# Attention of a dense masked transformer layer: scores of two heads at a time on the two halves of the array's rows, in place of one head on all 128

## The chip, the cores and the metric

The kernel runs on one core of one Trainium2 chip. The time is the device time of one execution in microseconds (us), and the number compared is the median of several runs. The core has a tensor engine (PE; its weight loads are listed apart as PEld), a vector engine (DVE), a scalar engine (ACT), GpSimd (POOL) and a queue (SP) that issues the DMAs. Each of them works off its own list of instructions in order, and they wait for one another by semaphores.

## What is computed

A graph attention network of two layers over 1250 nodes, then a graph transformer of two layers over the same edges. The change lies in the transformer. Cut to what matters:

```
N, D, H, DH, L = 1250, 512, 8, 64, 2
for l in range(L):
    q = ((x @ Wq[l].T + bq[l]) * scaling).reshape(n, H, DH)
    k = (x @ Wk[l].T).reshape(n, H, DH)
    v = (x @ Wv[l].T).reshape(n, H, DH)
    scores = jnp.einsum('ehd,ehd->eh', q[tgt], k[srcidx])
    m = segment_max(scores, tgt);  p = jnp.exp(scores - m[tgt])
    w = p / (segment_sum(p, tgt)[tgt] + 1e-16)
    agg = segment_sum(w[:, :, None] * v[srcidx], tgt)
    attn = agg.reshape(n, D) @ Wo[l].T + bo[l]
    x = _batchnorm(x + attn, ...)
    ff = relu(x @ W1[l].T + b1[l]) @ W2[l].T + b2[l]
    x = _batchnorm(x + ff, ...)
```

The kernel does not go edge by edge. It computes all 1250 x 1250 scores of a head and adds a matrix of logarithms of edge counts (`logs`, very negative where there is no edge), so that the softmax over all nodes is the softmax over the edges.

## The kernel before

**Stages.** A front stage counts edges, a stage computes the graph attention, and then each transformer layer has two stages: `stage_project_attend` (projections of x to k, q and v, then attention) and `stage_tail` (output projection, feed-forward, norms). A final stage normalises. In the profiled execution the projections of layer 0 run from 790 to 878 us and its attention from 878 to 1166 us; for layer 1 the attention runs from 1324 to 1612 us. The two attentions are the same program on other data.

**Two-part numbers.** A product that needs more precision than one pass gives is made of `high` and `low` parts (F32R each). Attention before the change uses the 64 channels of a head twice: `k_halves` holds k_high of a head in one half of the 128 partitions and k_low in the other (for odd heads the other way round), `q_first` and `q` (shown as `q_att` in the profile) hold q_high, copied to both halves of the partitions, and q_low, likewise. A matmul over all 128 rows then gives q_part·(k_high + k_low), and two of them, over q_high and q_low, give the score.

**Getting there.** `project_parts` works through five chunks of 250 nodes: k (48 matmuls), q (48), v (24). `save_k` (L1690) writes k_high by two copies of 64 partitions, `cut_k` (L1811) makes k_low by two subtractions, and SP stores k_low into the other half of the partitions (`store_k`). q goes out to the DRAM tensor `q_rows` (`store_q`) and comes back duplicated and reordered (`q_first_loaded`; later chunks by `load_q` in `attend_sync`).

**Attention.** A unit u is one head of one tile of 125 target nodes; there are 80 units a layer, two in a row make a pair p, 40 pairs a layer. For each unit:

- `score(u)` on PE (L2019): three column pieces of 512, 512 and 226 keys, twice, into three PSUM banks that all units share. It waits until unit u-1 is masked.
- `mask(u)` on DVE (L2125): reads the scores, adds `logs`, writes `probs`, and takes the row maximum.
- `exponential(u)` on ACT (L2073), then `safe` (L2130) and `divide` (L2134, L2136) on DVE.
- `turn(u)` on PE (L2029): ten transposes of 125 x 125 in three pieces of 4, 3 and 3, each piece into one bank. Before the change four banks go round (`RING = 4`, banks 3 to 6); a piece waits until the copy has emptied the bank of the piece four back.
- `save_turned(u)` on ACT (L2081): three copies out of these banks.
- `weigh(p)` on PE (L2040): for each of ten tiles one matmul for each of the pair's two heads, 64 weights' columns each, the even head into PSUM partitions 0 to 63 and the odd one into 64 to 127 of bank 7. The profile lists each of these F32 matmuls as two records, 40 a pair.
- `save_att(p)` on ACT (L2088) copies the result out.

The order on each engine is written out by hand. On PE it is turn(2p), turn(2p+1), score(2p+4), weigh(p-1), score(2p+5); DVE masks unit u+1 before it divides unit u; ACT does save_turned of both units, exponentials of units 2p+3 and 2p+4, save_att(p-1). On ACT and DVE eight cuts of the next stage's weights (`cut_w` L2094, `lower_w` L2142) are spread over pairs 16 to 30.

Of the kernel before, what the change touches and what calls it, by code (L numbers as in the profile page):

```python
# [1421 lines left out]
class LayerBuffers:  # L1422


    def __init__(self, k, ctx, gat, base, hidden):
# [6 lines left out]
        self.k_halves = base  # L1432
        self.q_out = base + 4 * H * N
        self.wk = gat.HIDDEN
        self.x_high = self.wk + 2 * weight
        self.x_low, self.k_low = self.x_high + x_size, self.x_high + 2 * x_size
        self.y, self.v_rows = gat.ROWS, gat.ROWS + gat.HALF
        self.q_first = gat.ROWS + 2 * gat.HALF
        self.wq = self.q_first + 8 * H * W
# [3 lines left out]
        self.w1, self.wo = self.q_out, self.x_high  # L1443
        self.w2 = self.wo + 2 * weight
        self.bias_rows = self.w1 + 8 * C * F * 128
        self.q_second = self.wk
# [23 lines left out]
def project_parts(k, ctx, places, x, x_cols, sources, weights, ready, loaded, bq, q_rows, q_first, k_halves, v_rows, logs, log_rows,  # L1470
# [18 lines left out]
    q_out = at("q_out", [128, 2, C, W], F32R, places.q_out)  # L1489
    k_low = at("k_low", [128, 2, C, W], F32R, places.k_low)  # L1490
# [6 lines left out]
    k.q_stored = nc.alloc_semaphore(f"q_stored{k.layer}")  # L1497
    k_stored = [k.sem(f"k_stored{slot}_qkv{k.layer}") for slot in range(2)]
    x_stored, prefetched = k.sem(f"x_stored_qkv{k.layer}"), k.sem(f"prefetched_qkv{k.layer}")
    q_first_loaded = k.sem(f"q_first_loaded_qkv{k.layer}")  # L1500
# [12 lines left out]
    k.q_saved, k.k_summed, k.k_low_done, k.v_summed, k.v_saved, k.k_stored = q_saved, k_summed, k_low_done, v_summed, v_saved, k_stored  # L1513
    k.q_first_loaded, k.first_logs_loaded, k.cols_stored = q_first_loaded, prefetched, x_stored
# [9 lines left out]
    def v_bank(t):  # L1524
        return k.psum[0:P, (4 + t) * BANK:(5 + t) * BANK]
# [7 lines left out]
    def own(odd):  # L1533
        return slice(odd * CH, (odd + 1) * CH)

    def nodes(s):
        return slice(s * W, (s + 1) * W)

    def k_at(rows, odd, s):
        return k_halves[own(rows)].rearrange("p (c odd) n -> p odd c n", odd=2)[:, odd][:, :, nodes(s)]  # L1540

    def project_sync(sp):
# [15 lines left out]
        def store_k(r):  # L1558
            sp.wait_ge(k_low_done, r + 1)
            for odd in range(2):  # L1560
                sp.dma_start(k_at(1 - odd, odd, r).bitcast(F32), k_low[own(odd), r % 2].bitcast(F32)
                             ).then_inc(k_stored[r % 2], 16)

        def store_q(r):
# [10 lines left out]
        if closing:  # L1575
            for t in range(A):
                store_rows(t)
        store_k(0)
        store_q(0)
        if closing:  # L1580
            for t in LATE:
                store_rows(t)
# [1241 lines left out]
```

## Time and profile before

| | |
|---|---|
| median of 3 runs | 1726.2 us (1725.1 to 1726.7) |
| span of the profiled execution | 1723.2 us |
| PE busy | 1572.0 us (91%) |
| DVE busy | 1300.9 us (75%) |
| ACT busy | 1177.9 us (68%) |
| POOL busy | 55.2 us (3%) |
| mean granted TensorE clock | 0.962 |

The profiled execution has a span of 1723.2 us from its first to its last instruction, 3.0 us less than the median of the timed runs; what lies around it is start and end of the program. How to read it: "busy" is time in which an engine has at least one instruction in it, and for PE the ends of matmuls are modelled, so starts of matmuls are what to measure by. The granted clock is a share of 2.4 GHz. A row of the timeline merges instructions of one kind that follow each other ("x20"); its first number is the start of the first.

### The profile page before, as it was taken

The page shows a single profiled execution, that of the slowest core. Times are in us where ns is not written, and L with a number is a line of the kernel's source. Part 1 is how long each engine was busy: PE and PEld are TensorE (multiplying, and loading weights), DVE is VectorE, ACT ScalarE, POOL GpSimd, SP SyncE. Part 2 cuts the span into 40 slices and gives each one's busy share as a digit, 9 for nine tenths or more (in the row PEclk, how much of TensorE's full clock was granted, in tenths as well). Part 3 has the DMA queues.
Part 4 walks back from the last instruction along what each step waited for, and adds up shares of the span by engine and source line. Part 5 has one row for each costly group of instructions (what it writes and reads, how often), then busy time and mean ns, then how long its engine had stood idle before and what let it go on. Part 6 is the DMA issues. An engine that isn't in the chain of part 4 may idle for free. (4 is left out here: it accounts for less than half of the span.)

```text
span 1723.2 us, 35023 instructions
## 1 busy us (share of the span) xinstructions
PE 1572.0 (91%) x14122; PEld 1429.3 (83%) x14122; DVE 1300.9 (75%) x2269; ACT 1177.9 (68%) x2181; POOL 55.2 (3%) x67
## 2 busy tenths in 40 slices
PE   7899799999995888798989999998799999999982
PEld 3788799999975777787978888888798888888882
DVE  6996999989468999995357777766733777777577
ACT  3455788888656999896457788873434777887434
POOL 0000000000000100000001000001100000000030
PEclk9899899999997999899999999999899999999995
DMA  4113222300006321112955333004067333200501
GB/s 180 55 53 101 83 70 76 122 31 2 1 1 176 120 91 61 61 32 86 245 151 150 91 89 85 16 2 134 1 158 205 94 78 78 64 2 1 123 5 59
DMA packets 76435, 139.33 MB, mean 81 GB/s; under 512 B 16849, under 2 KB 50353, under 8 KB 74992
## 3 DMA queue, kind: packets, MB, share of 16 engines
q1 hardware_dynamic: 76272, 137.06, 28.2%
q8 instruction: 114, 1.87, 0.5%
q14 instruction: 49, 0.40, 0.1%
HBM read 96.22 MB, written 29.45 MB: 73 GB/s over the span
## 5 line engine op out<-in xcount | busy, mean ns | idle before, releaser
L2125 DVE CUSTOM_DVE_ANT_0 probs_att<-banks,logs_or_y 125x1250 f32<-125x1250 f32 x160 | 233.6, 1460 | 124.9 <-PE banks L2019 123.5
L1028 PE MATMUL banks<-ident,probs_gat 125*125 125x125 f32 x1600 | 214.1, 283 | 46.7 <-ACT probs_gat L1132 46.1
L2081 ACT COPY probs_t_att<-banks 125x375 f32<-125x375 f32 (+1 forms) x480 | 205.0, 532 | 72.1 <-PE banks L2029 72.1
L2073 ACT ACTIVATE probs_att<-probs_att,neg_max_att 125x1250 f32<-125x1250 f32 x160 | 218.4, 1365 | 48.5 <-DVE neg_max_att L2125 48.5
L1028 PEld LDWEIGHTS banks<-ident,probs_gat 125*125 125x125 f32 x1600 | 194.7, 195 | 57.3 <-ACT probs_gat L1132 57.1
L1132 ACT ACTIVATE probs_gat<-probs_gat,neg_max_gat 125x1250 f32<-125x1250 f32 x160 | 214.7, 1342 | 34.3 <-DVE neg_max_gat L1301 33.8
L1301 DVE CUSTOM_DVE_ANT_0 probs_gat<-probs_gat,log_counts 125x1250 f32<-125x1250 f32 x160 | 236.8, 1480 | 0.1
L2040 PE MATMUL banks<-probs_t_att,v_rows 125*64 125x125 f32 x3200 | 189.5, 272 | 0.9 <-ACT feature_cols L2088 0.9
L2029 PE MATMUL banks<-ident,probs_att 125*125 125x125 f32 x1600 | 189.3, 273 | 0.0
L1039 PE MATMUL banks<-h,probs_t_gat 125*125 125x128 f32 x1600 | 188.9, 274 | 0.0
L2040 PEld LDWEIGHTS banks<-probs_t_att,v_rows 125*64 125x64 f32 x3200 | 170.6, 136 | 19.5 <-ACT probs_t_att L2081 17.7
L2029 PEld LDWEIGHTS banks<-ident,probs_att 125*125 125x125 f32 x1600 | 181.3, 189 | 4.7 <-DVE probs_att L2136 0.3
L1039 PEld LDWEIGHTS banks<-h,probs_t_gat 125*125 125x125 f32 x1600 | 182.1, 189 | 0.0
L2136 DVE TENSOR_SCALAR probs_att<-probs_att,inverse_att 125x1250 f32<-125x1250 f32 x160 | 140.1, 876 | 5.6
L1143 ACT COPY probs_t_gat<-banks 125x1250 f32<-125x1250 f32 x120 | 142.9, 1191 | 1.0 <-PE banks L1028 0.7
L2019 PE MATMUL banks<-k_halves,q_first 128*125 128x512 f32 (+1 forms) x576 | 134.3, 368 | 9.4 <-DVE neg_max_att L2125 7.9
L1295 DVE SCALAR_TENSOR_TENSOR probs_gat<-a_pair,a_dst_gap 125x1250 f32<-125x1250 f32 x80 | 121.3, 1517 | 21.5 <-PE banks L1028 12.0
L1295 DVE SCALAR_TENSOR_TENSOR probs_gat<-a_pair,a_dst_gap_gat 125x1250 f32<-125x1250 f32 x80 | 120.8, 1511 | 8.8 <-DMA a_pair<-a_src_rows 5.7
L2019 PEld LDWEIGHTS banks<-k_halves,q_first 128*125 128x125 f32 x576 | 92.7, 187 | 32.7 <-DVE neg_max_att L2125 9.9
L2019 PE MATMUL banks<-k_halves,q_att 128*125 128x512 f32 (+1 forms) x384 | 89.6, 368 | 0.0
L547 PEld LDWEIGHTS banks<-offset_hot,key_hot_fr 125*125 125x125 bf16 x650 | 76.0, 143 | 15.6 <-DVE offset_hot L361 7.0
L547 PE MATMUL banks<-offset_hot,key_hot_fr 125*125 125x250 bf16 x650 | 81.7, 280 | 7.2 <-issue 7.1
(258 smaller groups left out, 2892.9 us busy)
## 6 DMA issues: line engine op xcount, KB each, us to landing
a_pair<-a_src_rows SPq DMA_DIRECT2D x46, 625.0 KB, 4.8
q_first<-q_rows SPq DMA_DIRECT2D x12, 1000.0 KB, 11.2
logs_or_y<-log_rows SPq DMA_DIRECT2D x20, 546.9 KB
q_rows<-q_out_qkv SPq DMA_DIRECT2D x40, 250.0 KB, 4.6
q_att<-q_rows SPq DMA_DIRECT2D x8, 1000.0 KB, 10.8
w_rows<-in_L_gnn_W_dram SPq DMA_DIRECT2D x12, 512.0 KB, 13.7
log_counts<-counts_fr SPq DMA_DIRECT2D x50, 122.1 KB
k_halves<-k_low_qkv SPq DMA_DIRECT2D x20, 250.0 KB, 3.9
```

The source lines that it names most:

```text
L547: product = pe.matmul(sums(g), key_hot[:, g % 2, r, 0:P], offset_hot[:, (first[g] + r) % RING], start=r == 0, stop=r == R - 1)
L1028: block_t = pe.transpose(turned(u)[:, i // 2, (i % 2) * P:(i % 2 + 1) * P], probs[:, u % PROBS, i * P:(i + 1) * P], k.ident[0:P, 0:P])
L1039: total = pe.matmul(out_bank(u), probs_t_slot(u)[:, i], rows, start=i == 0, stop=i == T - 1)
L1132: act.activation(probs[:, u % PROBS], probs[:, u % PROBS], ACT.Exp, scale=-1.0, bias=neg_max[:, column(u)], accum_out=sums[:, column(u)]). ...
L1295: dve.scalar_tensor_tensor(probs[:, u % PROBS], gat.pair[0:P, head % 2, 0], (gat.gap1, gap2)[layer][:, t, head:head + 1], gat.pair[0:P, he ...
L1301: dve.tensor_tensor_reduce(probs[:, u % PROBS], probs[:, u % PROBS], k.log_counts[:, t], -1.0, -FLOOR, ALU.add, ALU.min, neg_max[:, column ...
L2019: total = pe.matmul(scores[:, a:a + width], q[r % 2][:, h, half, t % 2 * P:(t % 2 + 1) * P], k_halves[:, h, a:a + width], start=half == 0, ...
L2029: block_t = pe.transpose(turned(u, j)[:, (i - lo) * P:(i - lo + 1) * P], probs[:, u % SLOTS, i * P:(i + 1) * P], k.ident[0:P, 0:P])
L2040: total = pe.matmul(out_bank[odd * CH:(odd + 1) * CH], v_rows[:, i, h * CH:(h + 1) * CH], probs_t[:, u % TURNED, i], start=i == 0, stop=i ...
L2073: act.activation(probs[:, u % SLOTS], probs[:, u % SLOTS], ACT.Exp, scale=-1.0, bias=neg_max[:, column(u)], accum_out=sums[:, column(u)]). ...
L2081: act.copy(probs_t[:, u % TURNED, lo:hi].rearrange("p c n -> p (c n)"), turned(u, j)).then_inc(piece_saved, 1)
L2125: dve.tensor_tensor_reduce(probs[:, u % SLOTS], scores, logs[:, t % KEPT], -1.0, -FLOOR, ALU.add, ALU.min, neg_max[:, column(u)]).then_inc ...
```

## The change

The score of a pair is computed at once, by 18 matmuls over 64 rows each: the nine of the even head read partitions 0 to 63, the nine of the odd head partitions 64 to 127. They are q_high·k_high, q_high·k_low and q_low·k_high for each of three column pieces (q_low·k_low is no longer computed). The scores of a pair take 2500 columns, five banks; the odd head's pieces are 512, 452 and 286 wide, the even head's 226, 512 and 512, and the two share bank 2 (`shared_done` keeps the odd head's matmuls out of it until the even head's are done). The matmuls of the two heads are listed by the column at which each would begin if both heads streamed side by side.

k_high, k_low and q_high, q_low now stay where ACT and DVE write them, as [128, C, nodes]: a pair's two heads are already the two halves of the partitions. So `store_k`, `store_q`, the reload of q and their semaphores go, `save_k` and `cut_k` are one instruction each, and each chunk of q has a place of its own (`q_chunks`).

The three banks that are left (5, 6, 7) go round among seven tenants a pair: the six pieces of transposes and the result of `weigh`. A piece of an odd unit waits until the same piece of the even unit is copied out.

```
@@ attend_parts
-        def score(u):
...
-            for half in range(2):
-                for a, width in pieces(N):
-                    total = pe.matmul(scores[:, a:a + width], q[r % 2][:, h, half, t % 2 * P:(t % 2 + 1) * P],
-                                      k_halves[:, h, a:a + width], start=half == 0, stop=half == 1)
+        def score(p):
+            t, c = p // PER_TILE, p % PER_TILE
+            halves = q_chunks[t // 2][:, :, c, t % 2 * P:(t % 2 + 1) * P]
+            if p >= 1:
+                pe.wait_ge(masked, 2 * p)
...
+            for _, o, a, b, i in sorted(streams):
+                half, keys = ((0, k_high), (0, k_low), (1, k_high))[i]
+                if o == 1 and i == 0 and (a, b) == odd[-1]:
+                    pe.wait_ge(shared_done, p + 1)
+                total = pe.matmul(k.psum[0:P, a:b], halves[own(o), half], keys[own(o), c, a - o * N:b - o * N],
+                                  start=i == 0, stop=i == 2)
...
         def turn(u):
+            q, odd = u // 2, u % 2
             pe.wait_ge(divided, u + 1)
             for j, (lo, hi) in enumerate(CUTS):
-                if u * PIECES + j >= RING:
-                    pe.wait_ge(piece_saved, u * PIECES + j - RING + 1)
+                if odd:
+                    pe.wait_ge(piece_saved, 2 * q * PIECES + j + 1)
+                elif j < PIECES - 1 and q >= 1:
+                    pe.wait_ge(piece_saved, (2 * q - 1) * PIECES + j + 2)
+                elif q >= 2:
+                    pe.wait_ge(att_saved, q - 1)
...
         def weigh(p):
-            pe.wait_ge(piece_saved, (2 * p + 2) * PIECES)
-            if p >= 1:
-                pe.wait_ge(att_saved, p)
+            pe.wait_ge(piece_saved, (2 * p + 2) * PIECES + (PIECES + 1 if p + 1 < PAIRS else 0))
...
+        for p in range(PAIRS + 2):
+            if p < PAIRS:
+                score(p)
+            if p == 0:
+                by_rows(CHUNKS - 1, (1,))
...
+            if 1 <= p <= PAIRS:
+                turn(2 * p - 2)
+                turn(2 * p - 1)
+            if p >= 2:
+                weigh(p - 2)
@@ attend_scalar: save_turned(2p-2), save_turned(2p-1), exponential(2p), save_att(p-2), exponential(2p+1), cut_w
@@ attend_vector
+        for p in range(PAIRS):
+            mask(2 * p)
+            mask(2 * p + 1)
+            if p - 1 in cut_at:
+                lower_w(cut_at[p - 1])
+            for u in (2 * p, 2 * p + 1):
+                safe(u)
+                divide(u)
@@ project_parts
-            for odd in range(2):
-                saved = act.copy(like_banks(k_at(odd, odd, s)), by_feature(0)[own(odd)])
-            saved.then_inc(k_high_done, 1)
+            act.copy(like_banks(k_high[:, :, nodes(s)]), by_feature(0)).then_inc(k_high_done, 1)
```

The first score now also waits until the last chunk's q_low is made (`k.q_low_done`). The weights of the next stage are loaded in two parts (`rows_loaded` for Wo and W1 once eight pairs are scored, `last_rows_loaded` for W2 once 32 are), because W2 takes the place of a chunk of q; six cuts stand at pairs 16 to 26, two at pairs 35 and 36.

One pair on PE in the middle of a layer, before the change (L2029 turn, L2019 score, L2040 weigh):

```order
L2029 MATMUL banks<-ident,probs_att_10469 125x125 x3
L2029 MATMUL banks<-ident,probs_att_10469 125x125 [waits piece_saved_att0]
L2029 MATMUL banks<-ident,probs_att_10469 125x125 x2
L2029 MATMUL banks<-ident,probs_att_10469 125x125 [waits piece_saved_att0]
L2029 MATMUL banks<-ident,probs_att_10469 125x125 x2
L2019 MATMUL banks<-k_halves_10449,q_first_10452 125x512 [waits masked_att0]
L2019 MATMUL banks<-k_halves_10449,q_first_10452 125x512
L2019 MATMUL banks<-k_halves_10449,q_first_10452 125x226
L2019 MATMUL banks<-k_halves_10449,q_first_10452 125x512 x2
L2019 MATMUL banks<-k_halves_10449,q_first_10452 125x226
L2040 MATMUL banks<-probs_t_att_10470,v_rows_10450 64x125 [waits att_saved_att0,piece_saved_att0]
L2040 MATMUL banks<-probs_t_att_10470,v_rows_10450 64x125 x19
```

The end of a pair's scores and the beginning of the transposes behind them on PE with the change (L1982 score, L1999 turn):

```order
L1982 MATMUL banks<-k_high_10449,q_chunk_0_10453 125x286 [waits shared_done_att0]
L1982 MATMUL banks<-k_low_10450,q_chunk_0_10453 125x286
L1982 MATMUL banks<-k_high_10449,q_chunk_0_10453 125x512
L1982 MATMUL banks<-k_high_10449,q_chunk_0_10453 125x286
L1999 MATMUL banks<-ident,probs_att_10471 125x125 [waits divided_att0,total_step_fr]
L1999 MATMUL banks<-ident,probs_att_10471 125x125 x9
L1999 MATMUL banks<-ident,probs_att_10471 125x125 [waits piece_saved_att0,divided_att0]
L1999 MATMUL banks<-ident,probs_att_10471 125x125 x3
L1999 MATMUL banks<-ident,probs_att_10471 125x125 [waits piece_saved_att0]
```

Here it is the first pair, whose even unit finds all banks empty; the odd unit's first transpose waits for two semaphores, `divided` and `piece_saved`. Scores stood between the transposes and the weighing before; now all 20 transposes of a pair stand in a row, with the 20 matmuls of the weighing straight behind them.

Two units on DVE, before:

```order
L2125 ISA probs_att_10469,neg_max_att<-banks,logs_or_y_10451 125x1250 [waits piece_turned_att0,scored_att0]
L2125 ISA neg_max_att 125x1
L2130 TENSOR_SCALAR sums_safe_att<-sums_att 125x1 [waits exp_done_att0]
L2134 RECIPROCAL inverse_att<-sums_safe_att 125x1 [waits sum_safe_att0]
L2136 TENSOR_SCALAR probs_att_10469<-probs_att_10469,inverse_att 125x1250 [waits inverted_att0]
L2125 ISA probs_att_10469,neg_max_att<-banks,logs_or_y_10451 125x1250 [waits piece_turned_att0,scored_att0]
L2125 ISA neg_max_att 125x1
```

and with the change:

```order
L2084 ISA probs_att_10471,neg_max_att<-banks,logs_or_y_10452 125x1250 [waits piece_turned_att0,scored_att0]
L2084 ISA neg_max_att 125x1
L2084 ISA probs_att_10471,neg_max_att<-banks,logs_or_y_10452 125x1250 [waits piece_turned_att0,scored_att0]
L2084 ISA neg_max_att 125x1
L2089 TENSOR_SCALAR sums_safe_att<-sums_att 125x1 [waits exp_done_att0]
L2093 RECIPROCAL inverse_att<-sums_safe_att 125x1 [waits sum_safe_att0]
L2095 TENSOR_SCALAR probs_att_10471<-probs_att_10471,inverse_att 125x1250 [waits inverted_att0]
```

The two masks of a pair stand together, and the divisions of both units come behind them.

## Rows read from the trace of the kernel before

**Rows 1.** Busy by stretch: us; PE, PEld, DVE, ACT, POOL; clock; DMA; GB/s

```profile
20.00:45.00 25.00, 21.98 (x131) 13.71 (x129) 15.46 (x20) 12.65 (x31) 0.00 (x0) 1.00 0.19 57
810.00:850.00 40.00, 40.00 (x296) 37.55 (x295) 21.67 (x34) 21.69 (x35) 0.00 (x0) 1.00 0.71 172
899.00:1161.00 262.00, 262.00 (x2721) 234.77 (x2722) 196.76 (x381) 209.23 (x423) 16.12 (x18) 1.00 0.29 73
```

**Rows 2.** Timeline of PE, one pair (start us, us, engine, line, what, count)

```profile
936.17 1.42 PE L2019 MATMUL banks<-k_halves,q_att 128*125 128x512 f32 x6
937.42 2.35 PE L2029 MATMUL banks<-ident,probs_att 125*125 125x125 f32 x20
939.53 1.37 PE L2019 MATMUL banks<-k_halves,q_att 128*125 128x512 f32 x6
940.83 2.37 PE L2040 MATMUL banks<-probs_t_att,v_rows 125*64 125x125 f32 x40
943.13 1.42 PE L2019 MATMUL banks<-k_halves,q_att 128*125 128x512 f32 x6
```

**Rows 3.** Timeline of PE, beginning and end of layer 0's attention

```profile
878.51 1.42 PE L2019 MATMUL banks<-k_halves,q_first 128*125 128x512 f32 x6 [0.79 <-issue]
...
899.00 0.32 PE L2040 MATMUL banks<-probs_t_att,v_rows 125*64 125x125 f32 x1
...
1150.16 2.37 PE L2040 MATMUL banks<-probs_t_att,v_rows 125*64 125x125 f32 x40
```

**Rows 4.** Timelines of ACT and DVE in that pair

```profile
938.12 2.56 ACT L2081 COPY probs_t_att<-banks 125x500 f32<-125x500 f32 x6 [1.05 <-PE banks L2029]
940.51 1.39 ACT L2073 ACTIVATE probs_att<-probs_att,neg_max_att 125x1250 f32<-125x1250 f32 x1
...
937.62 1.46 DVE L2125 CUSTOM_DVE_ANT_0 probs_att<-banks,logs_or_y 125x1250 f32<-125x1250 f32 x1 [1.01 <-PE banks L2019]
```

**Rows 5.** Timeline of PE: an F32 matmul alone, and two on column halves

```profile
24.12 3.63 PE L573 MATMUL banks<-feature_cols,wa_fr 128*40 128x512 f32 x8
...
1045.61 0.33 PE L2040 MATMUL banks<-probs_t_att,v_rows 125*64 125x125 f32 x2
```

**Rows 6.** PE: starts of single matmuls, and one line's weight loads (min/median/max ns)

```profile
877.09 0.40 PE L1644 MATMUL banks<-wv_low,x_high_qkv 128*125 128x512 f32 x1
877.32 0.40 PE L1644 MATMUL banks<-wv_high,x_low_qkv 128*125 128x512 f32 x1
...
936.50 0.39 PE L2019 MATMUL banks<-k_halves,q_att 128*125 128x512 f32 x1
...
1160.71 0.27 PE L2029 MATMUL banks<-ident,probs_att 125*125 125x125 f32 x1
1160.91 0.33 PE L2040 MATMUL banks<-probs_t_att,v_rows 125*64 125x125 f32 x2
...
L580 PEld LDWEIGHTS banks<-ident,a_turned x10: 178/184/184, 37.5 to 38.5; 8*125 8x125 f32 x10
```

**Rows 7.** Timelines of PE, ACT and DVE where one waits for another

```profile
1158.29 0.37 PE L2029 MATMUL banks<-ident,probs_att 125*125 125x125 f32 x1
...
1159.08 0.58 ACT L2081 COPY probs_t_att<-banks 125x500 f32<-125x500 f32 x1 [0.41 <-PE banks L2029]
...
1158.70 0.87 DVE L2136 TENSOR_SCALAR probs_att<-probs_att,inverse_att 125x1250 f32<-125x1250 f32 x1
...
1159.63 0.37 PE L2029 MATMUL banks<-ident,probs_att 125*125 125x125 f32 x1
...
1163.33 0.26 ACT L2088 COPY feature_cols<-banks 128x125 f32<-128x125 f32 x1 [1.58 <-PE banks L2040]
...
1163.74 0.51 PE L2040 MATMUL banks<-probs_t_att,v_rows 125*64 125x125 f32 x5 [0.45 <-ACT feature_cols L2088]
```

**Rows 8.** DVE at the last chunk of q, and a DMA row (KB each, us to landing)

```profile
877.67 1.20 DVE L1817 TENSOR_TENSOR q_out_qkv<-q_qkv,q_out_qkv 128x1000 fp32r<-128x1000 f32 x1 [3.82 <-ACT q_out_qkv L1705]
...
q_first<-q_rows SPq DMA_DIRECT2D x12, 1000.0 KB, 11.2
```

More of the change, by code:

```diff
@@ L1907, in attend_parts @@
     PAIRS = UNITS // 2
+    PER_TILE, PER_CHUNK = H // 2, H
     KEPT = 4
@@ L1937, in attend_parts, with scores, columns, ring @@
         cuts += [(rows, high, low, a, a + step) for a in range(0, rows.shape[1], step)]
-    scored, masked, exp_done, sum_safe, inverted, divided, piece_turned, piece_saved, summed, att_saved = (
-        k.sem(f"{what}_att{k.layer}") for what in ("scored", "masked", "exp_done", "sum_safe", "inverted", "divided",
-                                          "piece_turned", "piece_saved", "summed", "att_saved"))
-    scores = k.psum[0:P, 0:N]
+    late = weights[-1][0].shape[1] * weights[-1][0].shape[2] // BANK
+    cut_at = {2 * PER_CHUNK + 2 * i: i for i in range(len(cuts) - late)}
+    cut_at.update({(CHUNKS - 1) * PER_CHUNK + 3 + i: len(cuts) - late + i for i in range(late)})
+    shared_done, scored, masked, exp_done, sum_safe, inverted, divided, piece_turned, piece_saved, summed, att_saved = (
+        k.sem(f"{what}_att{k.layer}") for what in ("shared_done", "scored", "masked", "exp_done", "sum_safe", "inverted", "divided",
+                                          "piece_turned", "piece_saved", "summed", "att_saved"))
+    def scores(odd):
+        return k.psum[0:P, odd * N:(odd + 1) * N]
+    def columns(odd):
+        lo, hi = odd * N, (odd + 1) * N
+        edges = [lo] + [b for b in range(0, 8 * BANK, BANK) if lo < b < hi] + [hi]
+        found = list(zip(edges, edges[1:]))
+        return found[-1:] + found[:-1] if odd == 0 else found[1:] + found[:1]
+    def ring(pair, tenant):
+        return (5 + (pair * TENANTS + tenant) % 3) * BANK
     def turned(u, j):
         lo, hi = CUTS[j]
-        at = (3 + (u * PIECES + j) % RING) * BANK
+        at = ring(u // 2, u % 2 * PIECES + j)
         return k.psum[0:P, at:at + (hi - lo) * P]
-    out_bank = k.psum[:, 7 * BANK:7 * BANK + P]
+    def out_bank(p):
+        at = ring(p + 1, 2 * PIECES)
+        return k.psum[:, at:at + P]
     def tile_of(u):
         return u // H
+    def own(odd):
+        return slice(odd * CH, (odd + 1) * CH)
     def column(u):
@@ L1957, in attend_sync @@
     def attend_sync(sp):
-        def load_q(r):
-            if r == 1:
-                sp.wait_ge(k.q_stored, 64 * (T // 2))
-                sp.wait_ge(k.k_summed, CHUNKS)
-            if r >= 2:
-                sp.wait_ge(scored, (r - 1) * 2 * H)
-            for copy in range(2):
-                sp.dma_start(q[r % 2][copy * CH:(copy + 1) * CH].bitcast(F32), q_rows[r]).then_inc(q_loaded[r % 2], 16)
         def load_logs(t):
@@ L2765, in build @@
                 sources = [[w[name][i] for name in ("Wk", "Wq", "Wv")] for i in range(layer, min(layer + 2, layers))]
-                k_halves = places.at(f"k_halves{layer}", [2 * CH, H, N], F32R, places.k_halves)
+                k_high, k_low = (places.at(f"k_{half}{layer}", [128, C, N], F32R, place)
+                                 for half, place in (("high", places.k_high), ("low", places.k_low)))
                 v_rows = places.at(f"v_rows{layer}", [P, T, D], F32, places.v_rows)
```

222 lines of the change are left out of this document (74 added, 148 removed).

## Prediction

> **What bounds the kernel now.** The page names PE the busiest engine at 91%, so I first asked for the busy time by stretch. In the attention of layer 0 PE is busy for 262.00 of 262.00 us while ACT is busy for 209 and DVE for 197, and in the projections for 40.00 of 40.00 us, ACT and DVE for some 22 each [rows 1]. The clock is granted in full (1.00, so 2.4 GHz) in both. Then the timeline of PE gives one pair by the starts of its phases [rows 2]: score 936.17 to 937.42 (1.25 us), 20 transposes to 939.53 (2.11), score to 940.83 (1.30), weighing to 943.13 (2.30), 6.96 in all. From the first weighing (899.00) to the one 36 pairs on (1150.16) it is 251.16 / 36 = 6.98 a pair [rows 3]. No phase waits: before the change attention costs what PE's list costs. A microsecond off PE counts only as far as PE does not begin to wait, since per pair ACT needs 209.23 / 262 x 6.98 = 5.6 us and DVE 5.2.
>
> **The change, part by part.**
>
> *Scores.* A pair has 2 x 2 x 1250 = 5000 columns to stream before, 1.25 + 1.30 = 2.55 us. Now it is 3 x 1250 = 3750 for each head, if the two heads stream side by side. No row of this trace has two matmuls on halves of the rows. The nearest is the weighing, two heads on halves of the columns. Eight F32 records of 512 columns, one at a time at the full clock, take 3.63 us [rows 1, 5], 0.45 each at most, so one of 125 columns would take 0.105 or a little more; 40 of them alone would be 4.2 us. The weighing's 40 take 2.30 [rows 2], and two start within the same 0.01 us [rows 5]. Halves of the columns do run side by side. From above the bound is no overlap at all, from below full overlap without any cost per matmul. I take full overlap with today's cost per matmul: 0.23 us for 512 columns and, where a matmul is short, 0.11, the distance of weight loads (877.09 to 877.32; ten loads in 1.0 us) [rows 6]. The even head has six of 512 and three of 226: 6 x 0.232 + 3 x 0.11 = 1.72. The odd head (512, 452, 286, three each) comes to the same by 0.45 ns a column, 1.70. A first matmul behind a change of the array's use costs 0.10 more (936.17 to 936.50 is 0.33, not 0.23), and so does the first behind a wait. Such a change also costs 0.09 ahead of it (1160.71 to 1160.91 is 0.20, where transposes are 0.11 apart) [rows 2, 6]. Before the change scores and transposes used the array alike; now they do not, so there are three changes a pair in place of two. Score phase: 1.72 + 0.10 + 0.09 = **1.91**, against 2.55: 0.64 less.
>
> *Transposes.* Twenty of them take 2.11 now. With three banks in place of four the odd unit's first piece waits until the even unit's first piece is copied out. From the first transpose behind a change to the beginning of that copy it is 0.79 (1158.29 to 1159.08), the copy takes 0.58 [rows 7], and PE goes on 0.15 later when, as here, it has two semaphores to wait for (the copy ends at 1163.59, PE starts at 1163.74), 0.06 when it has one (1159.57 to 1159.63) [rows 7]. So the odd unit starts 0.79 + 0.58 + 0.15 = 1.52 after the even one, where PE had been ready after ten transposes, 1.19. Then the weighing waits for the copy of the odd unit's first piece, since that bank is where its result goes: 0.79 + 0.58 + 0.06 = 1.43 more. **2.95** in place of 2.11: 0.84 more. Other pieces don't wait: the third bank's copies follow at 0.4 us each [rows 4], ahead of PE.
>
> *Weighing.* Twenty matmuls as before, **2.30**. It is no longer between two scores, but the change of use on either side is in it as before.
>
> *A pair.* 1.91 + 2.95 + 2.30 = **7.16** against 6.98, 0.18 more. Is another engine late? The second loop is weighing, copy of its result, exponential of the odd unit (behind that copy on ACT), its division, its transposes: 2.30 + about 0.25, 1.4 to 1.5, some 1.3 for the division (0.87 and two small instructions ahead of it), 0.06, and then 1.43 until the next weighing, 6.8 [rows 4, 7]. That is 0.35 less than 7.16, so it does not decide, but it is a floor: no gain in the scores can bring a pair under 6.8. The masks (1.46 each) lie beside the transposes.
>
> *Start of a layer.* Now 899.00 - 878.51 = 20.49 from the first score to the first weighing [rows 3]. The first score begins 0.4 later, since it waits for the last q_low, ready at 878.87 [rows 8]. Then, from it: scores 1.8; the last v, 12 matmuls of 0.23, until 4.7, its copy to 5.5; odd unit's exponential to 7.0 and division to 8.3; the masks of the next pair behind it on DVE, to 11.1; third scores to 13.0, beside them the exponentials and divisions to 14.3; transposes and copy 1.5: first weighing at 16.0. So 4.1 less a layer.
>
> *End of a layer.* Before, the last weighing starts 1163.74 - 878.51 = 285.23 after the first score [rows 3, 7]. With the change: 0.4 + 16.0 + 37 x 7.16 + 6.8 (the pair without scores, on the second loop) + 2.3 = 290.4. **5.2 us more a layer**, most of it 37 x 0.18 = 6.7, less 4.1 at the start, plus 2.6 at the end, where the pairs without scores used to be short.
>
> *At nothing:* one copy and one subtraction of k in place of two each, and the stores of k and q: PE is busy throughout the projections [rows 1], and if that cover went, ACT would save 1 us a chunk. The reload of q (12 DMAs of 1000 KB, 11.2 us each) [rows 8], since PE waits for nothing in a pair. The cuts of weights, eight a layer: 512 columns each, so about a copy's 0.58, and ACT has 7.16 - 5.6 = 1.5 us a pair to spare, most of it ahead of the first copy, DVE more behind its masks; uncovered they would be 8 x 0.6 = 5 us a layer. The first four tiles of the edge matrix are asked for no later than before, so the first mask does not wait for them.
>
> *Sum.* Two layers, 2 x 5.2 = 10: 1723.2 becomes 1733 in a profiled execution; the median stands 3.0 above the profiled span, so **1736**.
>
> **What decides.** Equal time needs 7.02 a pair, a score phase of 1.77. A measurement can tell 0.2%, 3.45 us or 0.05 a pair, from no change: below 1.72 it is faster, above 1.82 slower. My 1.91 is made of a borrowed cost per matmul.
>
> **Rivals.**
>
> *Faster: the halves hide each other's costs.* The 0.02 per matmul beyond its columns and the 0.10 of the first fall away when the other half streams: 3750 columns at 2.4 GHz are 1.56, and 0.09 gives 1.65. It speaks for this that the weighing's pairs of matmuls have next to no such cost (2.30 for 20 x 0.105). 0.26 x 37 x 2 = 19 less: 1717.
>
> *No change.* Half of that: a score phase of 1.72 to 1.82, or the waits for copies a tenth shorter: 1723 to 1730, say 1727.
>
> *Slower still: weight loads of the two halves go one behind the other.* 18 loads 0.11 apart are 1.98 in place of 1.72 [rows 6], 0.26 x 37 x 2 = 19 more: 1755. Against it: column halves load 0.01 apart. The Trainium skill ("TensorE: Matmul & The Clock Gate", Part 3, packing small matmuls) has four matmuls on quarters of the rows 3.07 times as fast as one by one, not 4; taken over as an estimate, 1.72 x 4 / 3.07 = 2.24 and the time some 1775. No run here shows that yet.
>
> *It does not do what it says:* matmuls on row halves run one after another. 1.72 + 1.70 = 3.42, 1.70 more for each of 40 pairs of two layers: 1736 + 136 = 1872. Only that column halves overlap speaks against it.
>
> **Chances.** Forecast (1730 to 1746) 0.45; faster 0.20; no change 0.17; serial loads 0.11; no overlap 0.07. So faster 0.20, same 0.17, slower 0.63. The range takes in both 1717 and 1755 with a little round them, 1713 to 1758, and leaves out no overlap and the tails, about 0.15.
>
> **What would show it.** The phases of a pair by their starts on PE: scores 1.9 until the first transpose, transposes 2.95 until the weighing, 2.3. A new wait of PE for ACT's copies (L1999 and L2008 for probs_t) of 0.3 + 0.15 a pair. Odd and even matmuls starting side by side in the scores. The first weighing 16 after the first score. I am wrong if scores take under 1.75 or over 2.0, or if PE takes the 20 transposes in under 2.7.

## Result: 0.3% to 0.6% slower, from the waits that were forecast, and less than was forecast

The changed kernel takes 1728.5 us (median of 20 runs, 1725.2 to 1734.5) beside 1725.2 us (20 runs) of the kernel before: the ratio is **1.0029, 95% interval 1.0019 to 1.0039**, so 5.0 us slower (3.3 to 6.7); the two medians are 3.3 us apart. One of the 20 runs of the kernel before took 2040.6 us and is left out of the ratio. Two later comparisons of the same two programs gave 1.0057 and 1.0046 (below). The forecast was 1736 us, 9.8 above the median shown before, a ratio of 1.0057, with a range of 1730 to 1746 (1713 to 1758 with the nearer rivals). The sign and the mechanism came true, the amount did not: 1728.5 lies under the 1730 to 1746 and inside the 1723 to 1730 that the prediction gave to "no change", and 5.0 us is half of the 9.8. The two later comparisons lie nearer to the forecast ratio, one of them on it.

The profiled execution of the changed kernel has a span of 1723.6 us, 0.4 more than before. That can't be read as "no change": the part of the program ahead of the first projection, which the change doesn't touch, took 785.5 us in this execution and 791.8 in that of before. From the first projection matmul to the end it is 938.1 against 931.4 us, 6.7 more. So I compare the changed stages with each other.

The busy time by stretch of the changed kernel (us; PE, PEld, DVE, ACT, POOL; clock; DMA; GB/s), projections and then attention, for [rows 1]:

```profile
810.00:850.00 40.00, 40.00 (x300) 37.73 (x300) 13.69 (x17) 17.55 (x28) 0.00 (x0) 1.00 0.39 105
890.00:1145.00 255.00, 247.02 (x2796) 222.23 (x2793) 189.20 (x367) 203.21 (x402) 13.84 (x16) 1.00 0.14 41
```

PE was busy in all of its time before; now 8 of 255 us are open, at the same full clock. In the projections DVE works 13.7 us of 40 in place of 21.7 and DMA's share halves, and PE's 40.00 show that this was worth nothing. Where the 8 us lie is seen in the timeline of PE, one pair, for [rows 2]:

```profile
934.34 0.49 PE L1982 MATMUL banks<-k_high,q_chunk 64*125 64x226 f32 x2
934.54 0.27 PE L1982 MATMUL banks<-k_low,q_chunk 64*125 64x226 f32 x1
...
935.93 0.39 PE L1982 MATMUL banks<-k_high,q_chunk 64*125 64x512 f32 x2
936.25 1.35 PE L1999 MATMUL banks<-ident,probs_att 125*125 125x125 f32 x10
937.76 1.32 PE L1999 MATMUL banks<-ident,probs_att 125*125 125x125 f32 x10 [0.16 <-ACT probs_t_att L2040]
939.15 2.37 PE L2008 MATMUL banks<-probs_t_att,v_rows 125*64 125x125 f32 x40
941.45 0.50 PE L1982 MATMUL banks<-k_high,q_chunk 64*125 64x226 f32 x2
```

Scores 934.34 to 936.25 (1.91), transposes to 939.15 (2.90), weighing to 941.45 (2.30): 7.11, and 7.12 as the median of all. The transposes are now two rows with a gap in front of the second, put down to ACT's copies. Those copies on ACT's timeline, for [rows 7]:

```profile
937.04 1.33 ACT L2040 COPY probs_t_att<-banks 125x500 f32<-125x500 f32 x3 [1.00 <-PE banks L1999]
938.52 1.32 ACT L2040 COPY probs_t_att<-banks 125x500 f32<-125x500 f32 x3 [0.15 <-PE banks L1999]
```

The first copy begins 0.79 us after the first transpose (936.25 to 937.04) and PE goes on 0.72 after that; the odd unit's copies begin 0.76 after 937.76, and the weighing 0.63 after them. The beginning and the end of layer 0's attention on PE, for [rows 3]:

```profile
871.73 0.40 PE L1599 MATMUL banks<-wv_high,x_low_qkv 128*125 128x512 f32 x1
873.42 0.50 PE L1982 MATMUL banks<-k_high,q_chunk 64*125 64x226 f32 x2 [1.29 <-DVE q_chunk L1764]
...
889.32 0.64 PE L2008 MATMUL banks<-probs_t_att,v_rows 125*64 125x125 f32 x7
...
1152.80 2.37 PE L2008 MATMUL banks<-probs_t_att,v_rows 125*64 125x125 f32 x40
1156.16 1.35 PE L1999 MATMUL banks<-ident,probs_att 125*125 125x125 f32 x10 [1.00 <-DVE probs_att L2095]
1158.15 1.35 PE L1999 MATMUL banks<-ident,probs_att 125*125 125x125 f32 x10 [0.63 <-DVE probs_att L2095]
1159.57 4.52 PE L2008 MATMUL banks<-probs_t_att,v_rows 125*64 125x125 f32 x80
```

The first weighing comes 15.90 us after the first score (20.49 before), 37 pairs take 263.48, and the pair without scores 6.77.

The costliest groups (busy, mean ns, then idle time of the engine in front of them and what ended it) have three lines that are new:

```profile
L1999 PE MATMUL banks<-ident,probs_att 125*125 125x125 f32 x1600 | 214.5, 281 | 15.8 <-ACT probs_t_att L2040 11.7 <-DVE probs_att L2095 3.4
L2008 PEld LDWEIGHTS banks<-probs_t_att,v_rows 125*64 125x64 f32 x3200 | 170.6, 136 | 19.8 <-ACT probs_t_att L2040 19.8
L1982 PEld LDWEIGHTS banks<-k_high,q_chunk 64*125 64x125 f32 x960 | 126.0, 183 | 19.7 <-issue 15.7 <-DVE neg_max_att L2084 4.0
```

11.7 us of PE's idle time end with ACT's copies. The real price is higher, since the modelled ends of matmuls cover part of each wait: by starts of instructions the transposes went from 2.11 to 2.90 a pair, 60 us over 76 pairs, and the scores gave 0.64 of each 0.79 back.

### The profile page after: what moved, and what is told of

Its sections match the earlier page's. It is cut to its first block and busy times, and to the rows that moved or that the text cites. A ratio compares the mean times of both kernels' runs of the same rounds, so it can differ in the third digit from the quotient of the medians.

```text
span 1723.6 us, 35777 instructions
## 1 busy us (share of the span) xinstructions
PE 1557.5 (90%) x14602; PEld 1419.2 (82%) x14602; DVE 1287.9 (75%) x2259; ACT 1176.5 (68%) x2171; POOL 54.3 (3%) x67
## 3 DMA queue, kind: packets, MB, share of 16 engines
q8 instruction: 117, 1.92, 0.5%
## 5 line engine op out<-in xcount | busy, mean ns | idle before, releaser
L2040 ACT COPY probs_t_att<-banks 125x375 f32<-125x375 f32 (+1 forms) x480 | 212.1, 515 | 82.8 <-PE banks L1999 82.4
L2084 DVE CUSTOM_DVE_ANT_0 probs_att<-banks,logs_or_y 125x1250 f32<-125x1250 f32 x160 | 226.5, 1453 | 4.6 <-PE banks L1982 4.6
L1999 PE MATMUL banks<-ident,probs_att 125*125 125x125 f32 x1600 | 214.5, 281 | 15.8 <-ACT probs_t_att L2040 11.7
L1999 PEld LDWEIGHTS banks<-ident,probs_att 125*125 125x125 f32 x1600 | 186.5, 188 | 43.2 <-issue 32.8
L1982 PE MATMUL banks<-k_high,q_chunk 64*125 64x226 f32 (+2 forms) x960 | 159.0, 366 | 5.3 <-DVE q_chunk L1764 2.6
L1982 PEld LDWEIGHTS banks<-k_high,q_chunk 64*125 64x125 f32 x960 | 126.0, 183 | 19.7 <-issue 15.7
L1982 PE MATMUL banks<-k_low,q_chunk 64*125 64x512 f32 (+1 forms) x480 | 130.9, 350 | 0.0
L2089 DVE TENSOR_SCALAR sums_safe_att<-sums_att 125x1 f32<-125x1 f32 x160 | 24.6, 154 | 133.0 <-ACT probs_att L2032 132.6
```

The costliest lines, as they stand in the source:

```text
L1982: total = pe.matmul(k.psum[0:P, a:b], halves[own(o), half], keys[own(o), c, a - o * N:b - o * N], start=i == 0, stop=i == 2)
L1999: block_t = pe.transpose(turned(u, j)[:, (i - lo) * P:(i - lo + 1) * P], probs[:, u % SLOTS, i * P:(i + 1) * P], k.ident[0:P, 0:P])
L2040: act.copy(probs_t[:, u % TURNED, lo:hi].rearrange("p c n -> p (c n)"), turned(u, j)).then_inc(piece_saved, 1)
L2084: dve.tensor_tensor_reduce(probs[:, u % SLOTS], scores(u % 2), logs[:, t % KEPT], -1.0, -FLOOR, ALU.add, ALU.min, neg_max[:, column(u)]).t ...
```

## Experiments

The theory: the two row halves of the array work side by side in full; the loss is PE waiting in the ring of three banks. Rivals: the loss comes from the scores in halves or from switching the array's use; or PE is not what decides any more.

### The ring alone, on the kernel before (before_ring3)

```
-    RING = 4
+    RING = 3
```

> The kernel before with the pieces of the turned scores in a ring of three banks instead of four, and nothing else changed: the ring's part of the change alone. Theory: the odd unit's first piece now waits for the copy of the even one's first, as in the changed kernel, 1.52 us after the turning began instead of 1.05, and nothing takes that back, since TensorE never waited before: a pair takes 6.98 + 0.45 = 7.43 us, 76 pairs make 34 us, 1759 us (ratio 1.020). If it is that much, the row halves give 7.43 - 7.12 = 0.3 us a pair or more back in the changed kernel. Rival (the ring costs nothing of itself, the loss comes with the scores in halves): 1725 us, ratio 1.000.

Measured: 1754.5 us, ratio 1.0166 (1.0150 to 1.0182), 28.6 us slower. PE's timeline:

```profile
1034.53 1.42 PE L2019 MATMUL banks<-k_halves,q_first 128*125 128x512 f32 x6
1035.79 1.25 PE L2029 MATMUL banks<-ident,probs_att 125*125 125x125 f32 x10
1037.20 1.32 PE L2029 MATMUL banks<-ident,probs_att 125*125 125x125 f32 x10 [0.16 <-ACT probs_t_att L2081]
1038.29 0.48 PE L2019 MATMUL banks<-k_halves,q_first 128*125 128x512 f32 x1
```

The odd unit starts 1.41 us after the even one (not 1.52: the first transpose follows scores that use the array alike, and is 0.10 cheaper), the transposes take 2.50 instead of 2.11, and the median pair 7.36 instead of 6.97. 76 x 0.39 = 30 us: one of the two waits, alone, costs four to six times what the whole change does. The rival that the ring is free falls.

### Smaller first pieces (cuts334, cuts244)

```
-    CUTS = ((0, 4), (4, 7), (7, 10))
+    CUTS = ((0, 3), (3, 6), (6, 10))
```

> The changed kernel with the scores of a unit turned in pieces of 3, 3 and 4 blocks instead of 4, 3 and 3; the same work. Theory (the changed kernel loses by the two waits in the ring of three banks, each of which ends with a copy of a first piece): the odd unit starts 1.28 us after the even one instead of 1.52 (three transposes to the landing of the piece 0.69, its copy 0.45, resuming 0.15), and the weighing is then held by ScalarE's four copies in a row (0.69 + 0.45 + 0.45 + 0.58 + 0.45 = 2.62, and 0.05): 2.67 us after the turning began instead of 2.90. A pair takes 6.88 us instead of 7.12: 76 steady pairs x 0.24 = 18 us less than the changed kernel, about 13 less than the one before, 1712 us. Rival 1 (the loss lies in the score phase or in switching the array's use, the copies are covered): a pair stays at 7.12, no change to the changed kernel, 1730 us. Rival 2 (ScalarE and VectorE have no more room): the weighing starts earlier, but the next score then waits for the masking, and less than 8 us of the 18 come out.

and with `CUTS = ((0, 2), (2, 6), (6, 10))`:

> The changed kernel with pieces of 2, 4 and 4 blocks; the same work. Theory (the waits end with copies of pieces): the odd unit doesn't wait at all (two transposes to the landing 0.58, copy 0.33, resuming 0.15 = 1.06, against ten transposes of 0.105 = 1.05), but its third piece waits for the copy of the even one's third (0.58 + 0.33 + 0.58 + 0.58 = 2.07), so the weighing starts at 2.07 + 0.15 + 4 x 0.105 = 2.64 us at the latest instead of 2.90. A pair takes 6.86 us, as much as pieces of 3, 3 and 4: 1711 us. Rival (the waits are not what holds TensorE): 7.12 us a pair, 1730 us.

Measured: 1714.4 us, ratio 0.9943 (0.9931 to 0.9955), and 1714.9 us, ratio 0.9941 (0.9928 to 0.9954). Both are faster than the kernel before. The same work, cut elsewhere, takes 0.86% off the first ratio of the changed kernel and 1.0% off the mean of all three (1.0044): 15 to 17 us, where 18 and 19 were expected. The median pairs are 6.90 and 6.91 us (expected 6.88 and 6.86); the timeline of cuts334 no longer breaks between the two units:

```profile
1013.13 2.76 PE L1999 MATMUL banks<-ident,probs_att 125*125 125x125 f32 x20
1015.83 2.37 PE L2008 MATMUL banks<-probs_t_att,v_rows 125*64 125x125 f32 x40
```

and its costliest groups say of the same line:

```profile
L1999 PE MATMUL banks<-ident,probs_att 125*125 125x125 f32 x1600 | 220.6, 286 | 3.7 <-DVE probs_att L2095 3.5 <-ACT probs_t_att L2040 0.2
```

Transposes 2.69 (expected 2.67), and of the 11.7 us behind ACT's copies 0.2 are left. That is by the modelled ends; by starts the odd unit still comes 1.30 us after the even one, 0.11 later than in the variants in which it does not wait (1.19). One part of my working was wrong: I had four copies in a row at their full durations, but they start only 0.36 to 0.54 us apart, so the copy of the odd unit's first piece ends 2.42 us after the turning began and holds nothing. What holds the weighing is the odd unit's last piece: it starts at 2.06, behind the end of the even unit's last copy (2.01), and its four transposes and the switch take the rest. In cuts244 it is the odd unit's second piece behind the even unit's second copy (1.53, start at 1.58), then eight transposes. Two different chains of nearly the same length.

### The same pieces on the kernel before (before_cuts334)

> The kernel before with pieces of 3, 3 and 4 blocks: a control for the pieces. TensorE waits for no copy there, so a pair stays at 6.98 us: 1725 us, ratio 1.000 within 0.2%. If smaller first pieces were a gain of themselves (shorter copies, an earlier weighing), it would be faster here too, by up to the 14 us that they brought the changed kernel.

Measured: ratio 1.0002 (0.9991 to 1.0014), and 6.97 us a pair, as before. The smaller piece is worth nothing where nothing waits for its copy; so its 15 us and more in the changed kernel are put down to the waits.

### Different pieces for the two heads (mixed)

```
-    CUTS = ((0, 4), (4, 7), (7, 10))
+    CUTS = (((0, 2), (2, 6), (6, 10)), ((0, 3), (3, 7), (7, 10)))
...
-        lo, hi = CUTS[j]
+        lo, hi = CUTS[u % 2][j]
```

> The changed kernel with the even head's unit turned in pieces of 2, 4 and 4 blocks and the odd head's in 3, 4 and 3; the same work. By the waits that pieces of 3, 3 and 4 and of 2, 4 and 4 showed (weighing 2.69 us after the turning began in both: held by the copy of the odd unit's first piece in one, by its third piece behind the copy of the even one's third in the other): here the even copies end at 0.58 + 0.33 + 0.58 + 0.58 = 2.07, the odd first piece's at 2.52, and the odd third piece of three blocks is turned by 2.07 + 0.15 + 0.32 = 2.54, so the weighing starts at 2.58. A pair takes 6.80 us, 8 us less than these two versions: 1706 us, ratio 0.989. Rival (VectorE and ScalarE are full by now, so the score waits for the masking instead): a pair stays at about 6.9 us, 1714 us, and the score shows idle time behind the mask.

Measured: 1707.6 us, ratio 0.9902 (0.9884 to 0.9921), 6.80 us a pair, the weighing 2.58 us after the turning began (expected 1706, 6.80 and 2.58). ACT and DVE were not full. One pair on PE's timeline:

```profile
1014.47 2.66 PE L1999 MATMUL banks<-ident,probs_att 125*125 125x125 f32 x20
1017.05 2.37 PE L2008 MATMUL banks<-probs_t_att,v_rows 125*64 125x125 f32 x40
```

and of the scores its groups say:

```profile
L1982 PE MATMUL banks<-k_high,q_chunk 64*125 64x226 f32 (+2 forms) x960 | 159.1, 366 | 5.5 <-DVE neg_max_att L2084 2.8 <-DVE q_chunk L1764 2.6
```

The score waits 2.8 us in all for the mask (2.6 in the changed kernel), so the rival falls. Three sizes of pieces and the control follow one sum: time of the transposes until the bank's next tenant may come.

### Do the row halves overlap, and does the order matter (serial, serial2, alternate)

The 18 score matmuls of a pair are sorted by the column at which each begins in its head's stream.

```
-                        streams.append((begin, o, a, b, i))
+                        streams.append((o * N + begin, o, a, b, i))
```

> The changed kernel with the nine matmuls of the even head all issued ahead of the nine of the odd head instead of by turns; the same work. Theory (the two row halves work at once only where matmuls of both are in the queue side by side): the score phase takes nearly twice its 1.72 us, 3.3 to 3.5 with the changes of array use, a pair 8.6 to 8.8 us, 76 pairs x 1.6 = 120 us more than the changed kernel: 1850 us, ratio to the kernel before 1.07. Rival (the halves don't overlap in the changed kernel either, and its 1.72 us come from something else): the order makes no difference, 1730 us.

Measured (two runs): 1747.9 us, ratio 1.0134 (1.0116 to 1.0152). The edit was not what its expectation says: a head's stream is 3 x N = 3750 columns long, so adding N puts the odd head's first matmul sixth in the program, not tenth. The 120 us were therefore no test. But the timeline showed something better (the odd head's first matmul is the first of 512 columns, the three of 226 are even):

```profile
1019.76 0.36 PE L1982 MATMUL banks<-k_high,q_chunk 64*125 64x226 f32 x1
1019.97 0.27 PE L1982 MATMUL banks<-k_low,q_chunk 64*125 64x226 f32 x1
1019.98 0.61 PE L1982 MATMUL banks<-k_high,q_chunk 64*125 64x512 f32 x3
...
1021.88 1.14 PE L1999 MATMUL banks<-ident,probs_att 125*125 125x125 f32 x8
```

The odd head's first, of 512 columns, starts 0.21 us after the even head's first, when only two even ones of 226 have started. In the program the third of 226 and two even ones of 512 stand ahead of it. The score phase is 2.11 us, longer by the 0.2 that the odd head starts later. With `3 * o * N + begin`, so all nine even ones first:

> The changed kernel with all nine matmuls of the even head ahead of the nine of the odd one; the same work. (In the run serial the odd head's first matmul was only the sixth in the program, and it started 0.21 us after the even head's first, ahead of three even ones that stand before it in the program; the score phase took 2.12 us instead of 1.92.) Theory A (the two row halves take their matmuls from queues of some depth each, and what is queued for one half doesn't block the other): the odd head starts when the ninth even one is taken up, and the phase grows by that delay, to 2.3 to 2.8 us: 76 pairs x 0.4 to 0.9 = 30 to 70 us more than the changed kernel. Theory B (only some three matmuls are looked past): the odd head starts when the even one's sixth does, 0.9 us in or later, and the phase takes 3.0 to 3.5 us: 80 to 120 us more.

Measured (two runs): 1799.5 us, ratio 1.0437 (1.0415 to 1.0459), 71 us above the changed kernel's 1728.5; a pair is 8.00 us, the score phase 2.80 (2.82 in the one shown):

```profile
1033.11 0.37 PE L1982 MATMUL banks<-k_high,q_chunk 64*125 64x226 f32 x1
1033.32 0.26 PE L1982 MATMUL banks<-k_low,q_chunk 64*125 64x226 f32 x1
1033.43 0.51 PE L1982 MATMUL banks<-k_high,q_chunk 64*125 64x226 f32 x2
1033.78 0.39 PE L1982 MATMUL banks<-k_low,q_chunk 64*125 64x512 f32 x1
1034.01 0.62 PE L1982 MATMUL banks<-k_high,q_chunk 64*125 64x512 f32 x3
...
1035.93 0.37 PE L1999 MATMUL banks<-ident,probs_att 125*125 125x125 f32 x1
```

Five even ones start at 33.11, 33.32, 33.43, 33.53 and 33.78, each half alone at 0.23 us for 512 columns. At 34.01 two start together, the sixth even one and the odd head's first, 0.90 us in. That is theory B's place (three matmuls are looked past: the seventh to ninth even ones start later) with theory A's price, because I had added theory B's up wrongly: 0.9 + 1.70 + 0.19 = 2.79, not 3.0 to 3.5. One half alone streams no faster than both together, so the overlap in the changed kernel is complete, and the rival that the halves run one after another falls by 0.9 us a pair.

```
-                        begin += b - a
+                        begin += 1
```

> The changed kernel with the matmuls of the two heads strictly by turns (first even, first odd, second even, ...), whatever their widths, instead of by the columns that each head has behind it; the same work. With strict order in the queue each step takes the wider of two matmuls, 226 beside 512 columns first and 512 beside 286 last: 9 x 512 columns' time of 0.213 = 1.92 us instead of 1.72, 15 us more over 76 pairs. If matmuls are looked past as in the run serial, the order by turns costs nothing: 0 +- 3 us.

Measured: 1729.8 us, ratio 1.0038 (1.0023 to 1.0053), the same pair of 7.12 us and the same starts of all 18 within 0.01 us. Sorting by columns is worth nothing here. A likely reason is that the order by turns too keeps each half's next matmul among the three that are looked past; no run tests this alone.

### The first score's wait (qwait), and both gains (qwait_mixed)

```
-        pe.wait_ge(k.q_low_done, CHUNKS)
+        pe.wait_ge(k.q_low_done, 1)
...
+            if p == PER_CHUNK:
+                pe.wait_ge(k.q_low_done, CHUNKS)
```

> The changed kernel with the first score waiting for the low half of the first chunk of Q alone, and the low half of the last chunk waited for where the second chunk's scores begin. The first score then starts with the last copy of Q out of its banks, as in the kernel before, 3.8 us after the projection's last matmul of Q instead of 4.4. VectorE still does that subtraction ahead of its first mask, so if the mask is what the start hangs on, nothing comes of the 0.6 us a layer; if the score is, 1.2 us in all: 1729 us, ratio 1.002 to 1.003.

Measured: 1726.5 us, ratio 1.0016 (1.0006 to 1.0025). The first score follows the last matmul of V at once and comes 3.00 us after Q's last in both layers, in place of 4.37:

```profile
872.55 0.40 PE L1599 MATMUL banks<-wv_high,x_low_qkv 128*125 128x512 f32 x1
872.88 0.50 PE L1984 MATMUL banks<-k_high,q_chunk 64*125 64x226 f32 x2
```

That is 1.37 us a layer, more than twice my 0.6, and the first weighing still comes 15.94 us after the first score, so nearly all of it arrives. My 3.8 was the distance in the kernel before, which I had put down to the last copy of Q out of its banks; without any other wait it is 0.8 us shorter. By the ratios the edit gains 2.2 us on the first comparison and 4.8 on the mean of three. The trace alone would not show it: from the first projection matmul to the end it reads 938.9 us, 0.8 more than the changed kernel's, with a stretch at half the clock behind the attention of layer 0 (see the last of the experiments).

> Both edits that gained, together: pieces of 2, 4 and 4 and of 3, 4 and 3, and the first score not waiting for the last chunk's low half. The pieces gave 6.80 us a pair (1707.6 us), the wait 1.36 us from the last matmul of Q to the first score in both layers. Together 1707.6 - 2.7 = 1705 us, ratio 0.989. If VectorE's first mask hides the wait once the pairs are shorter, 1707.6.

Measured: **1701.7 us, ratio 0.9872 (0.9848 to 0.9896)**, the fastest of all, 22 us under the kernel before; expected were 0.989 and 1705. From the first projection matmul to the end its trace reads 914.1 us, 2.6 less than that of mixed and 17.3 less than the kernel before. The times gain some 5 us more than this; 2.6 of them are that the profiled execution (1704.4 us) was slower than the median, what gives the rest isn't shown.

### The changed kernel again (after_again, after_third)

> The changed kernel once more, beside the kernel before on one chip: a second trace of it, and a second ratio. If the steady pairs are what decides, they read 7.12 us again and the ratio is 1.003 (+5 us); what differs between the two profiled executions outside the projections and the attention (6.3 us in the first pair of traces) is chance and comes out otherwise here.

> The changed kernel a third time. The first comparison gave the ratio 1.0029 (1.0019 to 1.0039), the second 1.0057 (1.0041 to 1.0073), with the same pairs of 7.12 us in both traces. If a comparison carries an error of its own beyond its interval, the third lands anywhere from 1.003 to 1.006; if the first or the second was an exception, near the other.

Measured: 1733.4 us, ratio 1.0057 (1.0041 to 1.0073), and 1731.6 us, ratio 1.0046 (1.0031 to 1.0062). The three traces of the same program from the first projection matmul to the end: 938.1, 941.5, 938.1 us, all with a median pair of 7.12. The 3.3 us more of the second are in layer 0, 1.7 between its first and its last weighing, most of that in the last two pairs, and 1.6 in the stage behind it. The busy time by stretch of after_again has the reason in the column of the clock, 0.50 (1.2 GHz) in two short stretches:

```profile
1161.20:1164.50 3.30, 3.30 (x26) 3.08 (x26) 0.00 (x0) 1.52 (x3) 0.00 (x0) 0.50 0.02 5
1171.50:1174.70 3.20, 3.20 (x17) 3.20 (x17) 1.46 (x3) 1.69 (x2) 0.00 (x0) 0.50 0.98 308
```

In the first trace the clock stands at 1.00 at the end of that attention and in the stage behind it, and PE had the same waits just ahead of the first of these stretches (1.00 and 0.63 us there, 0.99 and 0.63 here), so no trace shows why it fell. The kernel before has such stretches too, and one of them bears on the result. In before_cuts334 the clock falls to 0.50 while the first pairs of each layer fill up:

```profile
893.40:896.60 3.20, 3.20 (x13) 2.80 (x13) 1.96 (x2) 1.60 (x3) 1.01 (x1) 0.50 0.14 40
1340.60:1343.80 3.20, 3.13 (x11) 2.73 (x12) 1.75 (x6) 1.43 (x2) 0.00 (x0) 0.50 0.79 162
```

There the first weighing comes 22.05 and 21.93 us after the first score, 1.5 more than in the trace of before (20.49 and 20.48), and from the first projection matmul to the end it is 935.1 us in place of 931.4, with the same pair and, in the timed runs, the same time (ratio 1.0002). before_ring3 has it too in both layers; the changed kernel and its variants have it at neither start, in eleven traces. In the timed runs a lower mean clock goes with a longer time: of the changed kernel's 20 the two fastest (1725.2, 1725.4) have 0.967, the four slowest (1732.8 to 1734.5) 0.960 to 0.962. So one program carries a few us of its own from run to run, and an interval of 0.1% from one comparison is too narrow to hold for the next: the first and the second don't meet. The mean of the three ratios is 1.0044, 7.6 us.

## Why the prediction had the mechanism right and the amount too large

By its own steps, forecast against measured:

| step | forecast | measured |
|---|---|---|
| score phase | 1.91 | 1.91 to 1.92 |
| odd unit after the even one | 1.52 | 1.51 |
| weighing after that | 1.43 | 1.39 |
| weighing | 2.30 | 2.30 |
| transposes, both units | 2.95 | 2.90 |
| pair | 7.16 (before: 6.98) | 7.12 (before: 6.97) |
| first score to first weighing | 16.0 | 15.90, 15.92 |
| first score later | 0.4 | 0.5, 0.6 |
| pair without scores | 6.8 | 6.77 |
| more a layer | 5.2 | 3.6, 4.2 |

**Scores.** The borrowed prices (0.23 us for 512 columns, 0.11 for 226, 0.10 for the first, 0.09 for the switch) held: the first even and odd matmul start 3 ns apart, the last starts 1.68 us on, and the first transpose comes 0.23 later. The rivals "faster: the halves hide each other's costs" (1.65) and "serial weight loads" (1.98 and more) both fall by this number, and "it does not do what it says" by serial2. The prediction's estimate from the Trainium skill's 3.07 for four quarters ("TensorE: Matmul & The Clock Gate", Part 3) was 2.24; the trace shows no such loss for two halves of the rows.

**Waits.** Both stand where they were put, with the copies that were named. before_ring3 shows the first alone (0.39 a pair), the pieces shorten both, and before_cuts334 shows that nothing but the waits answers to the pieces.

**The step that failed** is the size of the waits: the term of the transposes, 2.95 in place of 2.11 (0.84 more a pair), measured 2.90 (0.79 more), so that a pair is 0.15 longer than before and not 0.18 (7.12 less 6.97). The working took 0.79 us for the odd unit's first piece too, but that is the time of a first piece behind a change of array use; behind a wait alone it is 0.76, and PE goes on 0.05 after a copy and not 0.06. 0.04 over 37 pairs is 1.5 us a layer. The smaller terms at the start and the end of a layer nearly cancel out, and layer 1 was 0.2 us shorter before the change than the layer 0 that the sum was worked out for, so 1.0 to 1.6 of the forecast's 5.2 a layer are too much. Two layers: 7.8 instead of 10.4 in the first traces.

**What stays open** is the step from there to the 5.0 of the first comparison. Everything outside the two attentions, which the sum put at nothing, is 1.1 us shorter in the trace of after than in that of before (6.7 against 7.8); one stretch at half the clock costs more than that. And the one trace of the kernel before happens to have no such stretch at the start of its attentions, where its near twin before_cuts334 has one in each, 1.5 us apiece. If the timed runs of the kernel before have them at times, the true difference is smaller than 7.8; how often they do isn't recorded. The mean of the three comparisons, 7.6, is close to 7.8, but with single comparisons from 5.0 to 9.8 that closeness is no proof. One slip has no weight in the ratio: the 3.0 us between profiled span and median are not all start and end of the program; each run stands only 1.8 above its own span (1725.4 against 1723.6 for the changed kernel).

**What decides** was stated as a score phase of 1.77 for equal time. With the scores as forecast the other side of that sum was the loose one: a tenth off the waits was named only as "no change", with a chance of 0.17. The waits came out a twentieth shorter (0.79 for 0.84), which with the smaller terms takes 2.6 us off the 1736; that the median of 1728.5 lies in the range of "no change" is more than this step explains. And 0.21 us off them made the kernel faster than before.

## What to carry to other kernels

When a change takes a buffer from a ring to give it to something else, price the ring before the gain: time from the first write of a piece to the end of the copy that empties it, against the work that the writer has in between. If it comes out longer, look at the size of the first piece before giving up the change: here cutting the same ten blocks elsewhere was worth 0.21 to 0.32 us a pair and turned a loss of 0.4% into a gain of 1%. Where the forecast difference is a few us, one trace of each kernel is not enough to size it: look at the granted clock of every stretch first. A chain of copies is to be summed by the distance of their starts and not by their durations.

## What the runs showed of the hardware

- Two matmuls on halves of the array rows start 3 ns apart and stream side by side without loss: 3750 columns for each half in nine matmuls take 1.68 us from the first start to the last, plus the last one's time, the same as one half alone would need (512 columns 0.23 us alone in serial2, as before the change [rows 6]).
- Matmuls did not start in the order of the program where they were on different halves of the rows: the odd head's first started with three even ones ahead of it still to come, in serial (0.21 us in) and in serial2 (0.90 us in) alike. The Trainium skill ("TensorE: Matmul & The Clock Gate", Part 3, the mechanism) says that matmuls start and end in program order and that only weight loads are pulled ahead; by that the score phase of serial2 would be 1.59 (start of the ninth even one) + 1.70 + 0.19 = 3.48 us, and the traces have 2.80. Here the measurement decides.
- The first transpose behind the scores in halves starts 0.23 us after the last of them (286 columns, 0.13 us of its own), and the next transpose 0.21 after that, where transposes are 0.11 apart otherwise: 0.2 us for this change of array use.
- The granted clock fell to 0.50 for a few us at a time, in places that differ between executions of the same program; each such stretch in the attention cost about 1.5 us (20.49 to 22.05 and 20.48 to 21.93 in before_cuts334, 1.7 in after_again).
- The copies of 375 columns on ACT last 0.48 us each and start 0.36 apart when they stand in a row.
